# A megakernel's engine orders made by another planner: longest path to the end, re-measured costs, and other fillings of TensorE's gaps

## What is computed

```python
x = x + attn_a(layernorm(x))   # a wavelet "attention": 8 + 8 + 1 shifts along the sequence
x = x + ffn(layernorm(x))      # mixture of 8 experts, top 1
x = x + attn_b(layernorm(x))   # a linear map, a tanh recurrence over 512 steps, layernorm
x = x + ffn(layernorm(x))      # the same experts again

# attn_a: gains = softmax(q @ W_qscale.T + scale_gain) over 11 scales; per scale j and tap tau
out += gains[j] * D4[tau] * sum_head(q * shift(k, tau << j)) * shift(v, tau << j)
out += softplus(bypass) * sum_head(q * k) * v
return (out * sigmoid(x @ W_gate.T + b_gate)) @ W_out.T + b_out
# attn_b: a scan, one step after the other
h = tanh(h @ A.T + x_t @ B.T);  y_t = h @ C.T
# ffn: expert e = argmax(x @ Wg.T) of each token; gelu(x @ W1[e] + b1[e]) @ W2[e] + b2[e]
```

## Time and profile before

| | us |
|---|---|
| three runs | 1431.16, 1432.24, 1438.38; median 1432.24 |
| span of the profiled execution, first instruction to last | 1436.4 |
| TensorE busy, matmuls | 1170.8 (82%) |
| TensorE busy, weight loads | 881.1 (61%) |
| VectorE / ScalarE / GpSimd busy | 796.3 / 651.3 / 788.6 |
| TensorE's mean granted clock | 0.858 |

### The profile page before, as it was taken

The page is one execution under the profiler, slowest core; times in us unless marked ns, Lnnn a source line. Parts: engine busy times, 40 slices in busy tenths (PEclk is TensorE's granted clock), DMA queues, the critical chain, the costliest instruction groups (busy, mean ns, idle before and its releaser), DMA issues. The chain is left out here.

```text
span 1436.4 us, 32831 instructions
## 1 busy us (share of the span) xinstructions
PE 1170.8 (82%) x9942; PEld 881.1 (61%) x9942; DVE 796.3 (55%) x1723; ACT 651.3 (45%) x2050; POOL 788.6 (55%) x1274
## 2 busy tenths in 40 slices
PE   3877886888888899789988899887899998995580
PEld 2644554566565666466655666676787777785570
DVE  4878788889966777576788647542122301240110
ACT  2233332465544664455554436363564344562250
POOL 2645458563776748862748844876315642324504
PEclk9989987999988998889999759788995567998895
DMA  4700001221221212111112221233332324444542
GB/s 126 213 1 0 1 1 47 61 65 58 86 66 44 64 44 70 51 51 38 44 46 86 60 63 46 77 97 105 108 104 77 98 83 123 118 132 121 146 116 60
DMA packets 117638, 107.58 MB, mean 75 GB/s; under 512 B 15540, under 2 KB 88541, under 8 KB 117469
## 3 DMA queue, kind: packets, MB, share of 16 engines
q1 hardware_dynamic: 106704, 88.01, 21.5%
q0 software_dynamic: 8192, 16.79, 3.9%
q10 hardware_dynamic: 2573, 0.69, 0.2%
HBM read 76.73 MB, written 28.70 MB: 73 GB/s over the span
## 5 line engine op out<-in xcount | busy, mean ns | idle before, releaser
L799 POOL TENSOR_TENSOR acc<-acc,term 128x512 f32<-128x512 f32 x219 | 281.5, 1286 | 71.9 <-DVE term L1341 54.8
L1160 PE MATMUL bank<-w,hT 128*128 x1088 | 217.5, 324 | 22.1 <-ACT hT L985 13.9
L1341 DVE TENSOR_TENSOR term<-bank,V 128x512 f32<-128x512 f32 x251 | 168.0, 684 | 67.2 <-PE bank L1110 44.0
L1005 ACT ACTIVATE hid<-bank 128x16 f32<-128x16 f32 x512 | 93.0, 182 | 243.6 <-PE bank L1187 203.0
L985 ACT ACTIVATE hT<-bank,b1T 128x128 f32<-128x128 f32 x544 | 165.2, 370 | 79.2 <-PE bank L1147 65.2
L839 POOL DMA_INDIRECT back<-sorted_y,slot_i x128 | 125.1, 978 | 135.8 <-DMA back<-sorted_y,slot_i 44.2
L1160 PEld LDWEIGHTS bank<-w,hT 128*128 128x128 f32 x1088 | 173.9, 221 | 41.1 <-issue 35.6
L1187 PEld LDWEIGHTS bank<-hid,abcT 128*32 128x32 f32 x4096 | 88.6, 116 | 162.2 <-ACT hid L1005 83.2
L1312 DVE SCALAR_TENSOR_TENSOR made<-bank,qkvb,K 128x512 f32<-128x512 f32 x251 | 176.2, 742 | 17.8 <-PE bank L1083 7.2
L1187 PE MATMUL bank<-hid,abcT 128*32 128x16 f32 x4096 | 138.6, 201 | 38.3 <-ACT hid L1005 37.1
L1147 PE MATMUL bank<-xTb,w1b 128*128 128x128 f32 x864 | 166.8, 321 | 3.2 <-ACT xTb L973 3.0
(11 more groups left out here) (177 smaller groups left out, 2153.4 us busy)
## 6 DMA issues: line engine op xcount, KB each, us to landing
w1b<-in_W SPq DMA_DIRECT2D x130, 256.0 KB
K<-in_W SPq DMA_DIRECT2D x54, 256.0 KB
xsb<-sorted_x SPq DMA_DIRECT2D x184, 64.0 KB
sorted_y<-ysb SPq DMA_DIRECT2D x136, 64.0 KB
X<-in_x SPq DMA_DIRECT2D x64, 64.0 KB
out_x<-X SPq DMA_DIRECT2D x64, 64.0 KB
sorted_x<-K SPq DMA_DIRECT2D x14, 256.0 KB, 3.6
sorted_y<-made SPq DMA_DIRECT2D x48, 64.0 KB
```

Of the source, the lines that this page charges most:

```text
L799: nc.gpsimd.tensor_tensor(acc[:], acc[:] if k > 1 else term[0][:], term[k % NTERM][:], ALU.add).then_inc(S["terms_added"], 1)
L1005: nc.scalar.activation(hid[n % 2][:, cs], bank[6 + n % 2][:, cs], ACT.Tanh).then_inc(S["h_ready"], 1)
L1160: last = nc.tensor.matmul(bank[SLOT_BANK[place(n)]][:, 0:D], tile(hT[place(n)], c), w2[:, ds(second[n] + c * D, D)], start=(c == 0), stop= ...
L1341: V_.tensor_tensor(term[k % NTERM][:], bank[2 + k % 2][:], V[:, at:at + CW], ALU.mult).then_inc(S["terms_ready"], 1)
```

## The change

The pieces of work stay the same: 2427 on TensorE, 1847 on ScalarE, 1205 on VectorE, 576 on GpSimd, 616 on SP, with the same arithmetic. Three things change.

1. *The costs.* Each piece gets two numbers: `pace`, after which its engine can begin the next, and `took`, after which its result is there; and `hop`, a time from one engine to another, is added between pieces of two engines. `PE_PACE` goes, engines begin at set times, a change of ScalarE's table, the pauses in GpSimd's rows of DMAs and a turn from other work to a step are counted.
2. *The choice.* For every piece the longest path from it to the end of the program is worked out (`to_go`). The engine that can begin first takes, among its pieces that are ready within 0.15 us, the one with the longest path, less 50 times what it would wait. Steps have no rank of their own.
3. *The fillings.* A count of streamed columns over the last 3.4133 us of the plan is kept; where it would be under 3300 at a piece's end, the planned gap ahead of it is filled with constant matmuls at 0.11 us each, also gaps under 0.5 us, and also in bank 0 between two owners. A bank counts as free 0.3 us after its last reader, before 1.0 us.

The built programs show 847 constant matmuls at 183 places for 486 at 83; 121 of the places wait for a bank's reader (21 before), 70 are in bank 0 (none before).

```diff
@@ planner @@
-PE_PACE = 0.93
-IDLE_US, FILL_US, FILL_SHARE, FREE_US = 0.5, 0.15, 0.65, 1.0
+Piece = namedtuple("Piece", "engine pace took after bank0")
+PACE = dict(
+    counts=(0.45, 0.60), gatep=(0.87, 1.02), kproj=(0.87, 1.02), vproj=(0.87, 1.02), qproj=(0.87, 1.02), logit=(0.82, 0.97),
...
+    loadw=(1.10, 3.75), loadx=(0.45, 2.25), store=(0.45, 2.25), outst=(0.62, 2.60))
+HOP = {("ACT", "PE"): 0.13, ("ACT", "DVE"): 0.03, ("PE", "ACT"): 0.05, ("PE", "DVE"): 0.04, ("DVE", "PE"): 0.06, ("DVE", "ACT"): 0.03}
...
+TABLE_US, TURN_US, LOOK_US, DAWDLE = 1.283, 0.11, 0.15, 50.0
...
-    for c in range(CHUNKS):
-            piece("PE", "step", c, k, 0.28, URGENT,
-                  [("state", c, k - 1) if k else past("state", c - 1, CT - 1), ("rxb", c, 0) if k == 0 else None])
+            piece("PE", "step", c, k, [("state", c, k - 1) if k else past("state", c - 1, CT - 1), ("rxb", c, 0) if k == 0 else None])
...
+    while ends:
+        key = ends.pop()
+        to_go[key] = max((hop(todo, key, y) + to_go[y] for y in followers[key]), default=todo[key].took)
...
-                choice = (at, todo[key][2], ready, key)
-                if pick is None or choice[0] < pick[0] - 1e-9 or (abs(choice[0] - pick[0]) < 1e-9 and choice[1:3] < pick[1:3]):
-                    pick = choice
...
+            if r <= now + LOOK_US:
+                choice = (DAWDLE * max(0.0, r - now) - to_go[key], key)
+                if best is None or choice < best[0]:
+                    best = choice, max(r, now)
...
+SPAN_US, TARGET, FILL_US, FILL_COLS, FREE_US = 3.4133, 3300, 0.11, 256, 0.3
...
-        if best and end and BEGIN[key] - best[0] > IDLE_US:
-            out[key] = int((BEGIN[key] - best[0]) * FILL_SHARE / FILL_US), best[1], best[2]
+        lack = TARGET - sum(c for _, c in recent) - columns_of(*key)
+        most = int((at - since) / FILL_US)
+        if end and lack > 0 and most > 0:
+            late = sum(since + FILL_US * j > stop - SPAN_US for j in range(most))
+            times = most - late + min(late, -(-lack // FILL_COLS))
+            out[key] = times, b, x
@@ TensorE @@
-                    if reader:
+                    if reader and b == 0:
+                        pe.wait_ge(S["bank0_taken"], filled)
+                    elif reader:
@@ after the fill @@
+                if (what, n, k) in TURN:
+                    filled = in_turn(what, n, k)
```

More of the change, by code:

```diff
@@ new lines, in cost @@
+def cost(what, n, k):
+    if what in ("hidden", "result"):
+        us = 0.222 * HC / parts(n)
+        return us, us + 0.17
+    if what == "gelu":
+        us = 0.25 * HC / parts(n)
+        return us, us + 0.12
+    if what == "spread" and terms(n)[k].g not in (0, 1):
+        return 0.87, 1.02
+    if what == "spread":
+        return 0.31, 0.47
+    if what == "scale" and k == 2:
+        return 0.21, 0.31
+    if what == "xmom" and STATS_GROUP[n][1] - STATS_GROUP[n][0] == 1:
+        return 3.16, 3.17
+    return PACE[what]
@@ L192, in past, with pieces, piece @@
+def pieces():
+    todo = {}
+    def piece(engine, what, n, k, after, bank0=None):
+        todo[what, n, k] = Piece(engine, *cost(what, n, k), [x for x in after if x is not None], bank0)
     def past(what, n, k=0):
         return (what, n, k) if n >= 0 else None
-    URGENT, USUAL = 0.0, 1.0
     for i in range(CHUNKS):
@@ L430, in fillings @@
+CLOSED_BY = dict(xT="xcopy", kproj="kcopy", vproj="vcopy", logit="shift", rows="rcopy", reduce2="pack2", gatep="tanh", out="resid",
+                 pT="pcopy", plog="plg", counts="ccopy")
 def fillings():
-    out, end = {}, 0.0
-    reader = {b: None for b in (1, 2, 3, 4, 5, 6, 7)}
+    out, end, recent = {}, None, []
+    last_of = {b: None for b in range(8)}
     for key in ORDER["PE"]:
         what, n, k = key
+        at, stop = BEGIN[key], BEGIN[key] + WORK[key].pace
         best = None
-        for b, last in reader.items():
-            since = max(end, BEGIN[last] + WORK[last][1] + FREE_US) if last else end
+        for b, x in last_of.items():
+            since = max(end or at, BEGIN[x] + WORK[x].took + FREE_US) if x else end or at
@@ L440, in fillings @@
             if best is None or since < best[0]:
[L441 to L445 removed]
+                best = since, b, x
+        recent = [x for x in recent if x[0] > stop - SPAN_US]
+        since, b, x = best
+        lack = TARGET - sum(c for _, c in recent) - columns_of(*key)
@@ new lines, in fillings @@
+        most = int((at - since) / FILL_US)
[3 more added lines that the diff above has]
+            out[key] = times, b, x
+            recent += [(since + FILL_US * j, FILL_COLS) for j in range(times) if since + FILL_US * j > stop - SPAN_US]
+        recent.append((at, columns_of(*key)))
+        if key in TURN:
+            last_of[0] = CLOSED_BY[what], n, k
+        elif what == "turn":
+            last_of.pop(SLOT_BANK[place(n)])
```

313 lines of the change are left out of this document (164 added, 149 removed).

## The result

Beside each other on one chip, the changed kernel took 1494.41 us (median of 4, 1474.88 to 1506.55) and the kernel before 1434.15 us (1431.16 to 1438.38): 1.035 times as long, 95% interval 1.025 to 1.045. Every ratio here goes by a kernel's fast runs alone, those not over 1.5% above its fastest (two of these four, 1486.43 and 1474.88), and so can differ from the ratio of the medians, which is 1.042 here. The forecast was 1277 us. The profiled execution is the longest of the four, 1506.55 us. A later kernel with the same order but the old filling rule, 1484.9 us from first to last instruction, has much the same picture in its scan stretch and its late signals (group 5).

A forecast was written before the change was run, and what follows sets the result against it. No engine was full: VectorE's order bounded attention, a step-tanh chain with TensorE's fixed order and clock the late scan, a scatter-slots-gather chain the end. 778 + 346 + 157 = 1281 us, forecast 1277 us; range 1195 to 1390 us.

The forecast's parts named there:

- B: Fifteenth residual to the scan's end: 383 steps plus two standstills, 346 us against 402 us before.
- "0.80 us" a step: Cost of a scan step after the fifteenth residual: 0.83 us read at the high clock, less 0.03; 306 us for 383.
- the two standstills: Scan stops between chunks 11 and 12 (13 slots, 25 us) and between chunks 13 and 14 (15 us).
- the boldest point: After the fifteenth residual, the scan's steps go by the rate of the high clock.
- R1: Rival: the clock stays low in the scan, 1.08 us a step, 454 us there, 1385 us in all; chance 0.18.
- A: Start to the fifteenth residual: 778 us against 862, with VectorE's 283 us of work after 433 us at density 0.82.
- C: Scan's end to the program's end: three TensorE waits for a `yadd` go, 157 us against 172.
- R3: Rival: fillings stand where no gap is, and 361 more are paid in full, 1325 to 1350 us; chance 0.08.
- R4: Rival: slots' turns wait on late loads and hold up TensorE's fixed order; 1461 us at 1 us more each; chance 0.08.
- R2: Rival: the last chunk reaches the scan late, its last 32 steps beginning at 1175 us; 1354 us in all; chance 0.14.
- The 0.88 for "faster": Chance given that the whole kernel gets faster by more than about 0.5%.

The follow-up runs named there:

- group 5: Copies on a chip with late signals, against before: changed order with old filling rule 1488.00 us (1.035); old order with changed filling rule 1430.21 us (0.995).
- group 4: Copies on a chip without late signals: changed kernel 1324.42 us, 0.934 of before's 1418.56 us; late or all scan steps first, 1323.45 and 1322.56 us.
- group 0: The result's own runs, on a chip with late signals: changed kernel 1494.41 us against 1434.15 us for the kernel before, 1.035.
- groups 0, 1 and 5: The groups with late signals; group 1 ran the changed order with the old filling rule, 1492.96 us (1.039), or without fillings, 1504.84 us (1.048).

## Why the prediction was wrong

**The step that failed is B's "0.80 us" a step.** The forecast was 346 us for 383 steps; the result has 529. By the starts of the steps in the trace, the two standstills of the order took 42.5 + 22.3 = 65 us (priced at 25 + 15), and the rest is 464 / 383 = 1.21 us a step. The text called it the boldest point: the price was read at the high clock, while the clock turned out at 0.72. R1 names that mechanism but prices it at 1.08 us, 1385 us in all, and gave it 0.18. The full price was beyond R1, because it also missed the late signals: those over 1 us cover 57 us of the 529, and (464 - 57) / 383 = 1.06 us a step is near R1's price. That is an estimate, as it puts all of the 57 us down to the steps. By it the low clock is the larger part of the loss in B, and the late signals themselves are the smaller.

Behind it stands a step that the prediction did not know it took: that times read from one chip's trace hold for an order that leans harder on the same engine. In the trace of before, 96 late signals cost little: 1434 us against 1419 in group 4. The stretches from modelled end to late signal come to 83 us there and to 130 us in the changed kernel. The old order's TensorE had 11 to 13% to spare in the scan stretch, the new order's 5% in group 4. That this is why the one order loses 170 us and the other 15 fits the windows, but is argued; I had no way to make signals late at will, nor to hold the clock.

**On the chip without them, point by point:**
- A, forecast 778 us: 770 (815 in group 0, late signals and 0.91 for 0.96 in the clock between). Right by luck, as its reason did not hold. VectorE was to keep 82% with 283 us of work; it did 251 us in 336 (75%). More of its work moved behind the fifteenth residual than the 16 us that I counted.
- B, forecast 346: 399. The standstills took 38.3 + 22.0 = 60 us for 40, the steps 339 / 383 = 0.885 us for 0.80. The mechanism is right here, and both terms are too small. In its densest place a step takes 0.61 us with a pair between:

```profile
941.34 0.26 PE L1269 MATMUL bank<-hid,abcT 128*32 128x16 f32 x8
941.53 0.49 PE L1242 MATMUL bank<-w,made 128*128 x2
941.96 0.26 PE L1269 MATMUL bank<-hid,abcT 128*32 128x16 f32 x8
942.15 0.49 PE L1229 MATMUL bank<-made,w1b 128*128 128x128 f32 x2
942.56 0.26 PE L1269 MATMUL bank<-hid,abcT 128*32 128x16 f32 x8
```

  so the mean of 0.885 is made by the steps behind several pieces, not by the usual one.
- C, forecast 157: 154, and 160 in group 0. Right on both, and by its reason: no turn in the last job waits over 2.3 us in either trace.
- The fillings, forecast to cost nothing: right. R3 falls; taking them out made each of the three orders tried slower, by 6 to some 20 us.
- R4, the turns: the turn's matmul waited 16.2 us for 184 turns in the changed kernel of group 0 against 43.8. It was the rival on the side where the result fell, and its mechanism did not occur.
- R2, the last chunk: its steps follow the chunk ahead of it by 0.8 us in group 0. It did not occur.
- The sum: 1277 us against 1324, inside the range; against 1494 it is far outside. That the forecast comes so near in group 4 is partly luck: A is right for another reason, and B's two terms are short by 53 us. The 0.88 for "faster" came true in group 4 and not in group 0.

## What to carry to other kernels

Before a loss is put down to an edit, run the changed kernel again at another time and on another chip, beside the kernel before: here 13% lay between two groups for the changed kernel, and 1% for the one before, so the kernel before is no control for this. Look for "remote" as the releaser in a one-core profile, and hold TensorE's semaphore events against the modelled ends of its matmuls: they tell of late signals that neither its busy time nor its clock shows. When experiments that undo different halves each cure all of the loss, suspect the comparison, not the kernel.

## What the runs showed of the hardware

TensorE's signals can come several us behind the modelled ends of its matmuls (up to 10.2 us for one signal), in part with the granted clock recorded at 1.00 (from 407.7 to 421.3 us in the changed kernel of group 0). There are 42 stretches and 130 us in all of such delay in that kernel, 30 and 83 us in before, none in group 4. Where several late signals end together they come 0.03 to 0.12 us apart, with matmuls between them that keep the signals at least 0.22 to 0.87 us apart in group 4, so the delay is at least in part the signal's own. The signals of the other engines were on time: VectorE, ScalarE and GpSimd had none over 1 us in these four traces. In kernels of the changed order with fillings the large stretches came at about the same work, near 413, 473, 551, 670 and 836 us in groups 0, 1 and 5. I did not find what starts them.

The clock goes with them: in the scan stretch the same instructions got 0.72 in group 0 and 0.96 in group 4, and in group 0 the clock fell to the lower level at 421.3 us, after TensorE had started nothing since 415.6 us. The two may feed each other (a late signal empties TensorE, an idle TensorE gets the lower clock, a slower one signals later), which no run here separates.
